# Attention over 16 sequences: weighed heads divided by their sums after a trip through DRAM, shifts computed on GpSimd

## The reference, cut to what matters

```python
x = x + layernorm(attention(layernorm(x)))   # 32 heads of 16 channels
x = x + layernorm(ffn(layernorm(x)))         # 512 -> 1408 -> 512, gated
# attention, for each head:
q, k = rope(h @ Wq.T + bq), rope(h @ Wk.T + bk)
v = h @ Wv.T + bv
w = softmax(causal(q @ k.T / 4))
out = concat(w @ v) @ Wo.T + bo
```

## Time and profile before

| | before |
|---|---|
| median of 3 runs | 2745.1 us |
| the profiled execution | 2745.2 us |
| its span, first to last instruction | 2743.5 us |
| attention phase in the span | to about 1720 us |
| PE busy over the span | 92% |
| DVE busy over the span | 77% |
| ACT busy over the span | 52% |
| POOL busy over the span | 36% |
| DMA packets | 236.66 MB, mean 86 GB/s |

### The profile page before, as it was taken

How to read it: one execution, slowest core, us unless ns; L and a number is a source line. 1 busy time by engine, 2 the same in 40 slices (tenths; PEclk the granted TensorE clock), 3 DMA queues, 4 the chain that set the end, 5 groups by cost and what they waited for, 6 DMA issues and landing times. The chain is left out here.

```text
span 2743.5 us, 55677 instructions
## 1 busy us (share of the span) xinstructions
PE 2519.6 (92%) x19584; PEld 1213.8 (44%) x19584; DVE 2122.0 (77%) x6399; ACT 1419.8 (52%) x1838; POOL 983.8 (36%) x1083
## 2 busy tenths in 40 slices
PE   3899999999999999999999996099999999999997
PEld 1444544444454454454454443044444444444443
DVE  5999999999999999999999994735555455555454
ACT  3576776776766666767676664322222222222221
POOL 4454655655565565555556553000000000000000
PEclk8999999999999999999999999599999999999999
DMA  5332433433333433433442330401121111121111
GB/s 170 98 95 76 125 92 99 122 104 94 115 105 92 117 104 92 121 102 95 123 118 77 106 96 32 191 16 46 46 76 46 46 61 46 46 76 46 46 46 46
DMA packets 125314, 236.66 MB, mean 86 GB/s; under 512 B 11441, under 2 KB 94897, under 8 KB 111921
## 3 DMA queue, kind: packets, MB, share of 16 engines
q1 hardware_dynamic: 123056, 232.84, 27.8%
q10 hardware_dynamic: 2048, 1.05, 0.1%
HBM read 148.39 MB, written 84.41 MB: 85 GB/s over the span
## 5 line engine op out<-in xcount | busy, mean ns | idle before, releaser
L655 DVE CUSTOM_DVE_ANT_0 mx<-mx,causal 128x512 f32<-128x512 f32 (+3 forms) x2048 | 944.3, 518 | 47.4 <-PE mx L785 43.4
L491 ACT ACTIVATE probs<-ts,exp_scale 128x1024 f32<-128x1024 f32 x640 | 708.8, 1107 | 325.7 <-PE ts L799 323.7
L1229 DVE SCALAR_TENSOR_TENSOR hidden<-gu,up_scale,silu 128x512 f32<-128x512 f32 x176 | 131.9, 750 | 417.7 <-PE gu L1279 407.9
L1088 ACT ACTIVATE silu<-gu,gate_scale 128x512 f32<-128x512 f32 x176 | 120.9, 687 | 631.4 <-PE gu L1279 631.4
L1063 POOL TENSOR_TENSOR f_rstd<-f_var,f_neg_half 128x4 f32<-128x4 f32 x32 | 32.3, 1009 | 928.8 <-DVE f_var L1206 647.3
L403 POOL TENSOR_SCALAR_AFFINE_SELECT probs<-probs 128x512 f32<-128x512 f32 x512 | 311.7, 635 | 145.2 <-ACT probs L491 145.2
L1277 PE MATMUL gu<-f_xT_hi,gate_hi 128*128 128x512 f16 x704 | 268.0, 381 | 51.9 <-issue 51.9
L813 PE MATMUL xb<-probs,vs 128*32 128x512 f32 (+3 forms) x4096 | 305.5, 439 | 5.0 <-ACT shift_rows L497 3.0
L382 POOL TENSOR_TENSOR turned<-biased,sin_sb 64x512 f32<-64x512 f32 x128 | 170.0, 1328 | 327.3 <-ACT biased L476 320.9
L655 DVE DVE_READ_ACCUMULATOR2_ANT row_max<- 128x1 f32 x2048 | 285.5, 139 | 0.0
L1279 PE MATMUL gu<-f_xT_lo,gate_hi 128*128 128x512 f16 x704 | 267.8, 380 | 0.0
(11 more groups left out here) (148 smaller groups left out, 4469.3 us busy)
## 6 DMA issues: line engine op xcount, KB each, us to landing
slots<-half SPq DMA_DIRECT2D x260, 128.0 KB, 12.6
qT<-slots SPq DMA_DIRECT2D x128, 256.0 KB, 3.8
kT<-slots SPq DMA_DIRECT2D x128, 256.0 KB, 4.0
xn<-x SPq DMA_DIRECT2D x16, 1024.0 KB, 9.1
xr<-x SPq DMA_DIRECT2D x16, 1024.0 KB, 6.9
slots<-half SPq DMA_DIRECT2D x256, 64.0 KB
x<-xr SPq DMA_DIRECT2D x16, 1024.0 KB, 10.8
f_xn<-x SPq DMA_DIRECT2D x16, 1024.0 KB, 4.8
```

The source lines that it names most:

```text
L491: nc.scalar.activation(probs[:, g % 2, u, :, :], ts[:, :, :], ACT.Exp, scale=exp_scale[:, 0:1]).then_inc(ts_read, 1)
L655: last = nc.vector.tensor_tensor_reduce(out=scores, in0=scores, in1=causal[:, T - P * (qt + 1):T], scale=1.0, scalar=-3e38, op0=ALU.add, o ...
```

## The change

- The weighed heads (`oT`) are no longer turned on PE and divided on DVE. SP writes them to DRAM (`send_weighed`, 256 KB a group), reads the 8 rows of sums of a tile of 8 heads back as 128x32 (`fetch_sums`), DVE takes the reciprocal of that (`reciprocal_of_sums`), SP writes it to DRAM (`send_recips`) and reads back both the weighed heads and the reciprocals, each head's row repeated on its 16 partitions (`fetch_weighed`). GpSimd multiplies the two (`average`), ACT makes the high half (`high_of_attention`) with v's bias added there, and DVE the low half. `turn_weighed`, `turn_attention` and `divide_by_sums` are gone, and the bank uses "o" and "a" with them.
- v gets no bias at its evacuation, and ACT evacuates it (`read_v`) in place of DVE.
- The shifts are computed by GpSimd in three instructions, one unit later than DVE did it, and the DMAs that place them are issued by SP in place of ACT.
- `cosine` reads the PSUM bank and adds the bias itself; it comes ahead of the step's maxima, still waits for ACT's `biased`, and now is what frees the bank.
- In unit 2 without a turned tile, `weigh` takes the bank that `turn_shift` had; a turned x tile takes it too.
- The output projection is in groups 4 to 7 in place of 3 to 6, v's tile 0 in group 3. Statistics, roots, normalisations, residual and the three 1 MB transfers move by one to five steps.
- SP fetches the slots one unit later (unit 3). POOL's loop over the sequences is written out, as those of PE, DVE and ACT were.

```diff
-        V_OR_OUT = (("v", 1, 0), ("v", 2, 0), ("v", 3, 0), ("out", 0, -1), ("out", 1, -1), ("out", 2, -1), ("out", 3, -1),
-                    ("v", 0, 1))
-        TURNED = (("x", 2, 1), ("x", 3, 1), ("a", 3, -1), ("a", 0, 0), ("x", 0, 2), ("a", 1, 0), ("x", 1, 2), ("a", 2, 0))
+        V_OR_OUT = (("v", 1, 0), ("v", 2, 0), ("v", 3, 0), ("v", 0, 1), ("out", 0, -1), ("out", 1, -1), ("out", 2, -1),
+                    ("out", 3, -1))
+        TURNED = (("x", 2, 1), ("x", 3, 1), None, None, ("x", 0, 2), None, ("x", 1, 2), None)
+        SUMS_AT = {1: (3, -1), 3: (0, 0), 5: (1, 0), 7: (2, 0)}
+        FETCHED = {0: (2, -1), 2: (3, -1), 4: (0, 0), 6: (1, 0)}
+        AVERAGED = {1: (2, -1), 3: (3, -1), 5: (0, 0), 7: (1, 0)}
...
-        STATISTICS_AT = {14: (0, 1), 15: (2, 3)}
-        VARIANCE_AT = 15
-        ROOT_AT = 16
+        STATISTICS_AT = {15: (0, 1), 16: (2, 3)}
+        VARIANCE_AT = 16
+        ROOT_AT = 17
         NORMALISE_AT = {19: (0,), 20: (1, 2), 21: (3,)}
...
-        NORMALISE1_AT = {0: (0,), 1: (1,), 4: (2,), 5: (3,)}
-        RESIDUAL_AT = {1: (0, 1), 6: (2, 3)}
+        NORMALISE1_AT = {5: (0,), 6: (1,), 9: (2,), 10: (3,)}
+        RESIDUAL_AT = {6: (0, 1), 11: (2, 3)}
...
-            r = g % 2
-            BANK_USES += [(("qk",) + QUERIES_KEYS[g], r), (("s", (g + 1) % NG, (g + 1) // NG), 1 - r), (TURNED[g], r),
-                          (("av", (g - 1) % NG, (g - 1) // NG), 1 - r), (("o", (g - 1) % NG, (g - 1) // NG), 1 - r),
-                          (V_OR_OUT[g], r)]
+            BANK_USES += [(("qk",) + QUERIES_KEYS[g], r), (("s", (g + 1) % NG, (g + 1) // NG), 1 - r)]
+            if TURNED[g]:
+                BANK_USES.append((TURNED[g], 1 - r))
+                r = 1 - r
+            BANK_USES += [(("av", (g - 1) % NG, (g - 1) // NG), 1 - r), (V_OR_OUT[g], r)]
+            r = 1 - r
...
-        FREED_BY = {"qk": (biased_ready, 8), "v": (v_read, NC), "out": (out_read, NT), "s": (shift_read, NG),
+        FREED_BY = {"qk": ((cosine_done, 8),), "v": ((v_read, NC),), "out": ((out_read, NT),),
...
+            def send_weighed(i, g):
+                ready, fetched = held(sp, NG * i + g + 1), held(sp, 32 * (NC * (i - 1) + g // 2 + 1))
+                sp.wait_ge(oT_ready, ready)
+                wait_if_any(sp, averaged_in, fetched)
+                sp.dma_start(weighed[g // 2, g % 2, :, :], oT[:, :]).then_inc(weighed_out, 16)
...
+            def fetch_sums(i, c):
+                written = held(sp, 16 * (NC * i + c))
+                sp.wait_ge(weighed_out, 16 * (NG * i + 2 * c + 2))
+                wait_if_any(sp, recips_out, written)
+                heads = weighed[c, :, :, :].rearrange("g (h r) t -> (g h) r t", r=32)
+                sp.dma_start(sums[:, :], heads[:, DH, :].rearrange("h (a k) -> h a k", k=8 * T // P)).then_inc(sums_in, 16)
...
+            def send_recips(i, c):
+                divided, fetched = held(sp, NC * i + c + 1), held(sp, 32 * (NC * (i - 1) + c + 1))
+                sp.wait_ge(recip_done, divided)
+                wait_if_any(sp, averaged_in, fetched)
+                sp.dma_start(recips[c], sums[:, :]).then_inc(recips_out, 16)
...
+            def fetch_weighed(i, c):
+                consumed = held(sp, NC * i + c)
+                sp.wait_ge(recips_out, 16 * (NC * i + c + 1))
+                wait_if_any(sp, aT_ready, consumed)
+                heads = weighed[c, :, :, :].rearrange("g (h r) t -> (g h) r t", r=32)
+                of_head = recips[c].rearrange("(h o a) k -> h o (a k)", h=8, o=1)
+                sp.dma_start(spread[:, :], of_head.broadcast_to([8, DH, T])).then_inc(averaged_in, 16)
+                sp.dma_start(averaged[:, :], heads[:, 0:DH, :]).then_inc(averaged_in, 16)
...
+                    if u == 4 and exists(i + (g - 1) // NG):
+                        send_weighed(i + (g - 1) // NG, (g - 1) % NG)
                     if u == 1 and exists(i + owner):
                         send_slots(i + owner, n)
+                    if u == 1 and g in SUMS_AT:
+                        c, of = SUMS_AT[g]
+                        if exists(i + of):
+                            fetch_sums(i + of, c)
+                    if u == 1 and g in FETCHED:
+                        c, of = FETCHED[g]
+                        if exists(i + of):
+                            send_recips(i + of, c)
+                    if u == 2 and exists(i + (g + 1) // NG):
+                        place_shift(i + (g + 1) // NG, (g + 1) % NG)
-                    if u == 2 and exists(i + owner):
+                    if u == 3 and exists(i + owner):
                         fetch_slots(i + owner, n)
+                    if u == 3 and g in FETCHED:
+                        c, of = FETCHED[g]
+                        if exists(i + of):
+                            fetch_weighed(i + of, c)
-                    if s == 8 and exists(i + 2):
+                    if s == 9 and exists(i + 2):
-                    if s == 9 and exists(i - 2):
+                    if s == 14 and exists(i - 2):
-                    if s == 14 and exists(i - 2) and exists(i - 1):
+                    if s == 19 and exists(i - 2) and exists(i - 1):
...
+            def shift_of_maxima(i, g):
+
+                pool.wait_ge(mx_read, NS * i + NU * (g + 1))
+                wait_if_any(pool, shift_full, NG * i + g)
+                nc.gpsimd.tensor_scalar(shift[:, :, :, :, 0], row_max[:, g % 2, :, :, :], -1.0 / SHIFT_UNIT, None,
+                                        ALU.mult).then_inc(shift_step, 1)
+                nc.gpsimd.tensor_scalar(row_shift[:, :, :, :], row_max[:, g % 2, :, :, :], -1.0 / SHIFT_UNIT, None,
+                                        ALU.mult).then_inc(shift_step, 1)
+                pool.wait_ge(shift_step, 2 * (NG * i + g + 1))
+                nc.gpsimd.tensor_tensor(shift[:, :, :, :, 1], row_shift[:, :, :, :], shift[:, :, :, :, 0],
+                                        ALU.subtract).then_inc(shift_ready, 1)
+            def average(i, c):
+                pool.wait_ge(averaged_in, 32 * (NC * i + c + 1))
+                nc.gpsimd.tensor_tensor(averaged[:, :], averaged[:, :], spread[:, :], ALU.mult).then_inc(averaged_done, 1)
...
+            def read_v(i, ct):
+                act.wait_ge(v_full, NC * i + ct + 1)
+                nc.scalar.activation(vs[:, ct, :, :, 0:DH],
+                                     xb[:, bank_of("v", ct), :].rearrange("p (t h d) -> p t h d", t=NT, h=8),
+                                     ACT.Copy).then_inc(v_read, 1)
...
             def read_weighed(i, g):
+                wait_if_any(act, weighed_out, 16 * (NG * i + g))
                 act.wait_ge(av_full, NG * i + g + 1)
...
+            def reciprocal_of_sums(i, c):
+                dve.wait_ge(sums_in, 16 * (NC * i + c + 1))
+                nc.vector.reciprocal(sums[:, :], sums[:, :]).then_inc(recip_done, 1)
...
-                nc.vector.tensor_tensor(aT_lo[:, place, :], xb[:, bank, :], aT_hi[:, place, :],
-                                        ALU.subtract).then_inc(aT_ready, 1)
+                nc.vector.scalar_tensor_tensor(aT_lo[:, place, :], averaged[:, :], bias_v[:, c:c + 1], aT_hi[:, place, :],
+                                               ALU.add, ALU.subtract).then_inc(aT_ready, 1)
...
-                nc.vector.tensor_tensor(roped[:, n % 2, :], biased[:, n % 2, :], cos_sb[:, :],
-                                        ALU.mult).then_inc(cosine_done, 1)
+                nc.vector.scalar_tensor_tensor(roped[:, n % 2, :], xb[:, bank_of("qk", n), :], bias_qk[:, which, ct:ct + 1],
+                                               cos_sb[:, :], ALU.add, ALU.mult).then_inc(cosine_done, 1)
```

196 lines of the change are left out of this document (96 added, 100 removed).

## The result

The changed kernel takes 2721.9 us (median of 4 runs, 2721.5 to 2726.0) against 2745.4 us (median) of the kernel before on the same chip: ratio 0.9919, 95% interval 0.9901 to 0.9936. It is faster, as forecast, but by 23.5 us and not by 75. Its profiled span is 2719.8 us. The time lies inside the forecast's range, in the rival "part of it is eaten" (2690 to 2735), which had 0.18.

A forecast was written before the change was run, and what follows sets the result against it. PE was taken to set the pace, DVE close behind and ahead in group 3. A 101.1 us sequence loses 10.2 and regains 4.8, so 95.7; 16 x 5.4 = 86 less, 11 more at the end: 2670 us, range 2620 to 2742.

The forecast's parts named there:

- part of it is eaten: Rival: late cosines, late averages and DMA queueing cost 1 to 4 us a sequence; 2690 to 2735 us, chance 0.18.
- (b): In the 4 groups with an x tile, `weigh`'s bank waits for `cosine`; taken as 0, up to 0.7 us times 4.
- (c): ACT gets `read_v`, 0.6 us four times; free in groups 1 to 3, adds 0.55 us to group 4's wait.
- (a): In all 8 groups the product or x tile waits for ACT's `read_shift`: 0.45 us times 8, 3.6 a sequence.
- the tail: After the last sequence the chain of transfers is exposed: 15.4 us against 2.1, 13 more, taken as 11.
- (d): In group 3 DVE still has four statistics; 0.7 us allowed, half of the wait they caused before.
- turnings gone: PE loses `turn_weighed`, 5.9 us a sequence, and `turn_attention`, 2.4 us a sequence.
- group 3's wait gone: The output projection no longer waits for DVE's low half, made four units ahead: 1.4 us a sequence gained.
- normalisations out of group 0: Normalisations ahead of ACT's bias in group 0 move to groups 1 and 2: 0.5 us a sequence gained.
- DVE's relief: DVE loses 13 of its 96 us a sequence and is no bound at 95.7, but for group 3.
- slower rival: Shifts arrive late on SP's queue behind slots and 1 MB transfers, 8 us a sequence: 2798 us; chance 0.14.
- first rival: More gained: ACT drifts ahead, the bank wait and group 4's wait vanish; 2588 us, half of it 2630; chance 0.15.

The follow-up runs named there:

- e1: Changed kernel with x1's variance (DVE) and root (GpSimd) one step later, behind the cosine; 2721.1 us.
- e11: e10 with e9's edit, the cosine taken from ACT's biased tile in SBUF; 2690.6 us.
- e3: Changed kernel with v evacuated by DVE as a plain copy in place of ACT's `read_v`; 2737.7 us.
- e4: Changed kernel with the DMAs that place the shifts issued by ACT, behind unit 2's exponential, in place of SP; 2717.7 us.
- e9: Changed kernel with the cosine read from ACT's biased tile in SBUF, behind the maxima, and the bank freed by the bias; 2720.8 us.
- e2: Changed kernel with shifts turned by PE ahead of the projection's second half and read by ACT ahead of the bias; 2726.5 us.
- e13: e10 with the shifts' DMAs left on SP, so the changed kernel with only the new order of work and transfers; 2709.4 us.
- e15: Changed kernel with the edits of e9 and e2 together, the shifts' DMAs still on SP; 2699.1 us.
- e10: Changed kernel with ACT's normalisations spread, x tile 0 turned in group 5, residual and 1 MB transfers later, shifts' DMAs on ACT; 2704.7 us.
- e12: e10 with the edits of e9 and e2: cosine from SBUF, shifts turned and read first; 2664.0 us, ratio 0.9702.
- e16: e12 with e1's edit, x1's variance and root one step later; 2684.0 us.

## Why the prediction was wrong

The direction, the mechanism of the gain and the prices of the instructions held. What failed are two terms of "what comes back to PE": (b), the wait for the cosine, put at nothing, and (c), ACT's added work, put at nothing outside group 4. The bank wait (a) and the tail were put a little too low, and (d) too high by 0.4. By the prediction's own steps, us a sequence:

| step | forecast | measured |
|---|---|---|
| turnings gone | 8.3 | 8.0 |
| group 3's wait gone | 1.4 | 1.6 |
| normalisations out of group 0 | 0.5 | 0.3 |
| (a) bank wait on the turned shifts | 3.6 | 4.0 |
| (b) the product waits for the cosine | 0 (to 2.8) | 1.8 |
| (c) ACT's work ahead of scores and x tiles | 0.55 | 1.4 |
| (d) group 3's statistics | 0.7 | 0.3 |
| a sequence | 95.7 | 98.6 |

The measured terms are my sorting of PE's waits and add up to within 0.3 us of the 2.5 that a sequence lost.

- Step (b), "It waits for the same bias, then about 0.66 us of DVE; the x tile's 0.59 us hides most of it. I take 0." The duration was right (0.746). What failed is that DVE was taken to be free when the bias is ready. In group 0 it has its maxima, the last statistics of x1 and the variance in hand, and the product waits 1.28 us, in group 6 0.49. e1 takes the variance away and 0.76 of it goes. Since the row on DVE's share was 95.7, a new step that PE waits on should have been priced with DVE's queue ahead of it and not with its duration alone.
- Step (c), "In groups 1 to 3 ACT waits there for the scores anyway". It does, with only the old work. The same change moved four normalisations into groups 1 and 2, where `read_v` comes too, and PE waits for exponentials in groups 1 to 3 (0.6 us) and for ACT at group 1's x tile (0.3). I had costed the move of the normalisations as a gain in group 0 and as nothing where they went. In group 4 the forecast was right in size: 0.89 + 0.55 = 1.44 forecast, 1.45 measured.
- (b) and (c) are the larger part of the 2.9 us a sequence, some 46 us in 16 sequences. With both undone (e11, which also has the shifts' DMAs on ACT) 31 of the 46 come back, and a sequence takes 96.4.
- The tail: 15.4 us of chain forecast, 17.0 measured. Send 3.4, sums 2.35, reciprocals 1.4 and the last fetch 6.6 (two issues, one behind the other, then 256 KB) are 13.7 and not 12.5. My deduction of 2 us, "the output projection already ran behind by groups", had no row behind it, and nothing of it came: from 13 more I should have stayed at 13. After the idle stretch PE's first nine matmuls run at half the granted clock (0.58 to 0.64 us for 0.38), and cost 1.9 us more. In all +15.9, 5 more than forecast.
- 2670 + 46 + 5 = 2721.
- POOL's shifts, SP's issue load and the cover of the shifts' DMA were as forecast, DVE's relief nearly (11 us a sequence for 13); the DMA engines' share came to 0.49 and not 0.56. The slower rival's point of decision was not reached, but e3 shows it near: with the 0.7 us evacuation of v on DVE four times a sequence, the shifts do come late in some. The Trainium skill, "DMA: Bandwidth & Descriptors", section "Queues, rings and completion order", has one ring for each of SP and ACT on every DMA engine. Giving the shifts ACT's (e4) was worth 4 us, with no wait of PE for them to remove, and for group 4 they took longer from issue to landing than on SP's (5.3 us, median, for 4.1); so the runs do not show the rule's overtaking, nor that the gain comes from it.
- The range's rival (2690 to 2735) named late cosines, late averages and DMA queueing. The late cosine is shown. POOL does wait for the averages (117.5 us in all), but no wait of PE in the stream names them. Queueing is worth 4 to 8 us, if all that the shifts' DMAs on ACT bring is that. The range's lower end, 2620, is called half of the first rival, which by the rival's own sum is 2630; nothing hangs on it.

The larger error is one of method. The forecast takes each wait as a term that can be added or left out. The runs show that they cannot be, one by one:

| edits on the changed kernel | us against it |
|---|---|
| cosine from SBUF (e9) | -1 |
| shifts first (e2) | +5 |
| ACT's order (e13) | -12 |
| cosine and shifts first (e15) | -23 |
| ACT's order and shifts' DMAs (e10) | -17 |
| the same and the cosine (e11) | -31 |
| the same, the cosine and shifts first (e12) | -58 |

So the gain that failed to come was not lost to a single cause. PE, ACT and DVE hand each other work in every unit, and a wait taken from PE makes it arrive earlier at a stretch where ACT or DVE has no gap, as ACT has none at the start of group 4. What e12 has left (0.98 us for DVE in group 0, 1.1 for ACT at the start of group 4, DVE busy 92%) points to DVE as the next bound on average and to ACT at that one place; neither was tested. Not tried: e12's tail, and e2 with e10's order but the new cosine.

## What to carry to other kernels

When a change moves work onto an engine that is not the bound, price it in the stretch where it lands, behind what that engine already has there: ACT at 73% on average was full for 7 us in one group, and another order of its work gave 12 us back. If two new waits stand one behind the other, removing one may show nothing (+5 and -1 us here), so try the pair (-23) before dropping either. A moved instruction can change its length by what it meets: 0.17 us became 1.11. A chain of transfers that is hidden in the stream is paid in full once at the end, link by link, together with the slower clock after the idle time.

## What had not been expected of the hardware

- In e16 a DVE instruction on 128x4 (`minus_mean`) took 0.83 to 1.11 us in all of its twelve cases, each beside a running GpSimd product, and 0.17 in e12, where GpSimd was idle each time.
- The same small DMA of the shifts lands 2.5 us after its issue in a quiet group and 4.1 us after it (median) for group 4, beside the 1 MB transfers. The 256 KB of weighed heads took 3.4 us at the quiet end and 6.8 beside the 1 MB store.
- The cosine with both inputs in SBUF, which took 1.32 us in the median in the kernel before, takes 0.73 in e12, 0.68 at best and 1.77 at most, with the same GpSimd products in the kernel: what it costs depends on when it meets them. From PSUM and SBUF it was 0.72 to 0.75 in all 128 cases. The low half with two inputs in SBUF took 0.98 us in the tail while GpSimd added the residual, 0.75 while it was idle, and 0.875 in the mean of the stream. The Trainium skill, "SBUF — State Buffer", section "Who interferes with whom", says that an instruction with two such inputs contends with a GpSimd instruction that reads SBUF; these rows agree.
- A reciprocal of 128x32 took 0.34 us, one of 128x16 0.25; GpSimd's instructions on 128x16 took 0.22 to 0.26 in the mean.
